# A cross-attention and MX-FFN kernel: a first pass over all batches, gate arithmetic once on 128 partitions, weight scaling on VectorE

## What is computed

```python
ig = (x @ Wi + bi); fg = (x @ Wf + bf)          # x = concat(q, k, v), per head
log_f_cum = cumsum(log_sigmoid(fg))
log_D = tril(log_f_cum[s] - log_f_cum[t]) + ig[t]
D = exp(log_D - max(log_D))
C = (q @ k.T / sqrt(dh)) * D
h = (C / (max(|C.sum(-1)|, exp(-max(log_D))) + EPS)) @ v
x = x + layernorm_per_head(h) * ln_scale
```

## Time and profile before

| | us |
|---|---|
| median of 3 runs (624.54 to 626.63) | 626.4 |
| the profiled execution, own time | 627.32 |
| its span, first to last instruction | 625.5 |
| start, to the first CT product | 38.5 |
| batch steps, to the end of the last CT product | 367.5 |
| from there to the first transpose of the FFN | 27.7 |
| FFN from there | 191.8 |

### The profile page before, as it was taken

How to read it: one execution, slowest core, us unless ns; L and a number is a source line. 1 busy time by engine, 2 the same in 40 slices (tenths; PEclk the granted TensorE clock), 3 DMA queues, 4 the chain that set the end, 5 groups by cost and what they waited for, 6 DMA issues and landing times.

```text
span 625.5 us, 10355 instructions
## 1 busy us (share of the span) xinstructions
PE 500.4 (80%) x2944; PEld 324.3 (52%) x2992; DVE 516.3 (83%) x759; ACT 379.1 (61%) x739; POOL 381.2 (61%) x359
## 2 busy tenths in 40 slices
PE   1768689679789779867868768457999999999994
PEld 1356575566566557745646565343444444444441
DVE  1257899999999999999999999947788888888882
ACT  2487786787877867867867876632333443343342
POOL 5456677778668758848858758763334344444443
PEclk9977877787777875878866957757999999999999
DMA  5330313212302312302311301001011111111120
GB/s 129 136 102 1 102 35 103 101 35 103 101 34 101 101 34 101 101 34 94 103 38 47 121 1 34 18 1 50 1 44 58 34 51 49 34 59 41 34 67 34
DMA packets 25479, 38.48 MB, mean 62 GB/s; under 512 B 4848, under 2 KB 8944, under 8 KB 25456
## 3 DMA queue, kind: packets, MB, share of 16 engines
q1 hardware_dynamic: 25456, 38.21, 18.8%
HBM read 29.82 MB, written 8.39 MB: 61 GB/s over the span
## 4 chain that ended last, share of the span: by engine, by line
PE 40%; DVE 33%; issue 13%; ACT 8%; POOL 4%; DVEq 1%; DMA 1%; POOLq 0%; ACTq 0%; SPq 0%
PE psA L1335 7%; PE psA L1344 7%; PE psC L1362 5%; PE psA L1171 4%; PE psA L1145 4%; DVE wam L887 3%; PE psC L1204 3%; PE psC L1113 3%; DVE CT L959 3%; DVE f L935 3%; DVE wn L915 2%; POOL wn L598 2%; PE psB L1354 2%; ACT Dt L694 2%; PE psC L1195 2%
## 5 line engine op out<-in xcount | busy, mean ns | idle before, releaser
L598 POOL TENSOR_TENSOR wn<-wq,ps 128x1024 bf16<-128x1024 bf16 x32 | 61.1, 1911 | 109.7 <-DVE wq L1088 109.7
L1171 PE MATMUL psA<-vp,CT 128*128 128x33 f32 x512 | 83.5, 321 | 24.3 <-DVE CT L959 24.1
L1171 PEld LDWEIGHTS psA<-vp,CT 128*128 128x128 f32 x512 | 80.6, 243 | 29.6 <-issue 15.5
L1145 PE MATMUL psA<-qbd,kT 128*128 128x512 f32 x128 | 71.6, 711 | 0.4 <-issue 0.4
L694 ACT ACTIVATE Dt<-psB,gT 128x128 f32<-128x128 f32 x256 | 70.9, 376 | 0.2
L494 POOL TENSOR_TENSOR wq<-wn,ws 128x1024 bf16<-128x1024 bf16 x24 | 45.9, 1911 | 38.4 <-DVE wn L916 38.4
L844 ACT ACTIVATE wy<-psB 128x1024 bf16<-128x1024 bf16 x32 | 32.7, 1023 | 59.1 <-PE psB L1354 58.5
L501 POOL TENSOR_TENSOR wy<-wm,wy 128x1024 f32<-128x1024 f32 x24 | 63.2, 2632 | 0.9 <-ACT wm L676 0.9
L1335 PE MATMUL psA<-WgT,xqT 128*128 128x512 bf16 x241 | 61.6, 395 | 2.3 <-ACT WdT L687 1.5
L1362 PE MATMUL psC<-WdT,wy 128*128 128x512 bf16 x248 | 60.1, 379 | 2.9 <-ACT wy L844 2.4
L1344 PE MATMUL psA<-WuT,xqT 128*128 128x512 bf16 x255 | 62.0, 386 | 0.2 <-issue 0.2
(11 more groups left out here) (130 smaller groups left out, 1103.3 us busy)
## 6 DMA issues: line engine op xcount, KB each, us to landing
xt<-in_x_dram SPq DMA_DIRECT2D x8, 512.0 KB, 4.8
ct<-in_ctx_dram SPq DMA_DIRECT2D x8, 512.0 KB, 3.4
wraw<-in_L_ffn_w_gate_dram SPq DMA_DIRECT2D x8, 512.0 KB, 4.1
wraw<-in_L_ffn_w_up_dram SPq DMA_DIRECT2D x8, 512.0 KB, 4.8
wraw<-in_L_ffn_w_down_dram SPq DMA_DIRECT2D x8, 512.0 KB, 3.8
xr<-in_x_dram SPq DMA_DIRECT2D x16, 256.0 KB, 2.7
x_scratch<-x SPq DMA_DIRECT2D x16, 256.0 KB, 2.1
wm<-x_scratch SPq DMA_DIRECT2D x16, 256.0 KB, 2.7
```

The source lines that it names most:

```text
L598: nc.gpsimd.tensor_tensor(blocks(pd[h][:, :]), blocks(pc[h][:, :]), spread(ps4[h][:, :], PB), ALU.mult).then_inc(pq_ready.sem, 1)
L1145: nc.tensor.matmul(psA[:, i4, :], kT[p][:, i4, c * P:(c + 1) * P], qbd[:, i4, :, :].rearrange("p j t -> p (j t)"), start=True, stop=True). ...
L1171: last = nc.tensor.matmul(psA[:, i4, j * VW:(j + 1) * VW], CT[n % 2][:, j * P:(j + 1) * P], vp[p][:, c, HPC * i4 + j, :], start=True, stop ...
```

## The change

Shapes, inputs and the FFN loop are the same. What changes is the attention stage:

- A first pass over all batches (`pre_step`) loads, normalises and transposes x and ctx, makes the gate products, and quantises one down-weight unit per batch. The transposed q and k of all batches stay in SBUF (qTa, kTa). x and ctx have two buffers each.
- `gates` now has tokens as output partitions: 16 products per batch with 32 columns (both gates of 16 heads). After the last batch the gates of all batches and heads are transposed once to 128 partitions (8 batches x 16 heads) x 256, and log-sigmoid, scans, split and exponentials run once on those. The split rows go through a DRAM scratch (gs_dram, 393 KB) and come back per batch as factors movt and statt in eight small transfers (`load_decay`); the carry factor goes through g5_dram (four transfers a batch, `load_carry`).
- A second pass (`step`) makes the eight score tiles. `qk` takes 16 products of 32 rows and 128 columns per chunk in place of the four block-diagonal ones, so qbd goes; the exponent of D comes from two products, including the part that was ScalarE's bias, so `exps` is one activation of 128x512. `inter` adds the state's part in PSUM with a scaled q (`carry_q`, on GpSimd), in place of `combine`. Head variance, norm, residual, statistics and rounding work on both chunks at once (128x1024). The reciprocal root of the head variance is one pow on GpSimd (128x32) in place of logarithm, exponential and a correction.
- Weight units: scaling and scaling back move to VectorE, the addition too (as part of two `scalar_tensor_tensor` of the rounding), the clamp is absorbed, and the rounding constant is one activation. GpSimd has no weight work left. Eight units are in the first pass, two in the gate stage, two per batch after that (gate and up).
- FFN buffers are parts of qTa and kTa.

The core of the diff, in the order GpSimd, ScalarE, VectorE, TensorE:

```diff
+        qTa = sb("qTa", [P, B, HC, S])
+        kTa = sb("kTa", [P, B, HC, S])
...
+            def carry_q(b):
+                gp.wait_ge(g5b_ld, 16 * HPC * b + 16 * HPC)
+                gp.wait_ge(inter_done.sem, inter_done.at(b, 0))
+                settle(gp)
+                nc.gpsimd.tensor_tensor(qs[:, :, :], qTa[:, b, :, P:S], g5b[:, :, :], ALU.mult).then_inc(qs_ready.sem, 1)
...
+            def head_rsqrt(b):
+                gp.wait_ge(hv_ready.sem, hv_ready.at(b, 1))
+                nc.gpsimd.tensor_tensor(sm[:, 4, :, :].rearrange("p c h -> p (c h)"),
+                                        sm[:, 3, :, :].rearrange("p c h -> p (c h)"), mhalf[:, :],
+                                        ALU.pow).then_inc(hr_ready.sem, 1)
...
+            def step(b, p, n, first, last):
+                if not first:
+                    head_rsqrt(b - 1)
+                    residual(b - 1)
+                    x1_rsqrt(b - 1)
+                if not last:
                     weigh(b + 1, 1 - p)
+                    carry_q(b + 1)
+                if not first:
+                    back_x(b - 1)
...
+            def round_const(w, p):
+                act.wait_ge(pow_ready.sem, pow_ready.unit(w))
+                nc.scalar.activation(wm[p][:, :], wm[p][:, :], ACT.Identity, scale=W_SLOPE,
+                                     bias=wbase[:, 0:1]).then_inc(m_ready.sem, 1)
...
+            def pre_step(b, p, n, first, last):
+                copy_T(b, 0)
+                copy_T(b, 1)
+                if not last:
+                    x_norm(b + 1, 1 - p)
+                round_const(b, p)
+                if not first:
+                    evac_down(b - 1, b - 1)
...
+            def step(b, p, n, first, last):
+                if not first:
+                    square(b - 1)
+                exps(b, 0)
+                exps(b, 1)
+                if not last:
                     copy_v(b + 1, 1 - p, 0)
...
+                exps(b, 2)
+                exps(b, 3)
+                evac_gate_up(2 * b + B + 1, 1, b)
+                if not last:
+                    round_const(2 * b + B + 2, 0)
+                exps(b, 4)
+                copy_h(b, 0)
+                if not first:
+                    x1_norm(b - 1)
+                exps(b, 5)
+                if not last:
...
                     copy_v(b + 1, 1 - p, 1)
+                exps(b, 6)
+                if not last:
+                    evac_gate_up(2 * b + B + 2, 0, b + 1)
+                exps(b, 7)
+                if not last:
                     copy_state(b + 1)
...
+                    round_const(2 * b + B + 3, 1)
+                copy_h(b, 1)
+                if not first:
+                    evac_xq(b - 1)
...
+            def w_front(w, p, n):
+                ve.wait_ge(w_ld[p], 16 * n + 16)
+                ch.link(reduce_blocks(blocks(wraw[p][:, :]), wam[p][:, :]))
+                ch.link(power(wam[p][:, :], ws4[p][:, :]))
+                ch.link(inverse(ws4[p][:, :], winv[p][:, :], INV_W))
+                nc.vector.tensor_tensor(blocks(wy[p][:, :]), blocks(wraw[p][:, :]), spread(winv[p][:, :], UB),
+                                        ALU.mult).then_inc(y_ready.sem, 1)
+
+            def w_pow(w, p):
+                ve.wait_ge(y_ready.sem, y_ready.unit(w))
+                nc.vector.tensor_scalar(wm[p][:, :].bitcast(I32), wy[p][:, :].bitcast(I32), EXPO, None,
+                                        ALU.bitwise_and).then_inc(pow_ready.sem, 1)
+
+            def w_round(w, p):
+                ve.wait_ge(m_ready.sem, m_ready.unit(w))
+                ch.link(nc.vector.scalar_tensor_tensor(out=wy[p][:, :], in0=wy[p][:, :], scalar=W_LOW, in1=wm[p][:, :],
+                                                       op0=ALU.max, op1=ALU.add))
+                ve.wait_ge(wT_mm.sem, wT_mm.unit_before(w, 2))
+                nc.vector.scalar_tensor_tensor(out=wq[p][:, :], in0=wy[p][:, :], scalar=W_HIGH, in1=wm[p][:, :],
+                                               op0=ALU.min, op1=ALU.subtract).then_inc(wn_ready.sem, 1)
+
+            def w_back(w, p):
+                ve.wait_ge(wn_ready.sem, wn_ready.unit(w))
+                nc.vector.tensor_tensor(blocks(wq[p][:, :]), blocks(wq[p][:, :]), spread(ws4[p][:, :], UB),
+                                        ALU.mult).then_inc(wq_ready.sem, 1)
...
+            def pre_step(b, p, n, first, last):
+                w_front(b, p, n)
+                if not first:
+                    w_round(b - 1, 1 - p)
+                if not last:
+                    x_stats(b + 1, *after(p, n))
+                if not first:
+                    w_back(b - 1, 1 - p)
+                w_pow(b, p)
...
+            def step(b, p, n, first, last):
+                if not last:
+                    w_front(2 * b + B + 2, 0, b + B // 2 + 1)
+                if not first:
+                    head_var(b - 1)
                 c_mult(b, 0)
                 c_mult(b, 1)
+                w_round(2 * b + B + 1, 1)
                 c_mult(b, 2)
+                if not first:
+                    head_norm(b - 1)
+                w_back(2 * b + B + 1, 1)
                 c_mult(b, 3)
+                if not last:
+                    w_pow(2 * b + B + 2, 0)
+                if not first:
+                    x1_stats(b - 1)
                 c_mult(b, 4)
+                if not last:
+                    w_front(2 * b + B + 3, 1, b + B // 2 + 1)
                 c_mult(b, 5)
+                if not last:
+                    w_round(2 * b + B + 2, 0)
+                if not first:
+                    x1_round(b - 1)
                 c_mult(b, 6)
+                if not last:
+                    w_back(2 * b + B + 2, 0)
                 c_mult(b, 7)
+                if not last:
+                    w_pow(2 * b + B + 3, 1)
...
+            def gates(b):
+                pe.wait_ge(tr_ev.sem, tr_ev.at(b, 2))
+                settle(pe)
+                for c in range(NCH):
+                    for k in range(2 * HC):
+                        src = (qTa if k < HC else kTa)[:, b, k % HC, c * P:(c + 1) * P]
+                        last = nc.tensor.matmul(gate_out[:, b, c, :], src, wgt[:, k, :], start=False,
+                                                stop=k == 2 * HC - 1, skip_group_check=True)
+                return last
...
+            def qk(b, c):
+                pe.wait_ge(h_ev.sem, h_ev.at(b, c))
+                settle(pe)
+                for i4 in range(HC):
+                    for j in range(HPC):
+                        r = slice(DH * j, DH * (j + 1))
+                        last = nc.tensor.matmul(psA[:, j, i4 * P:(i4 + 1) * P], kTa[r, b, i4, c * P:(c + 1) * P],
+                                                qTa[r, b, i4, c * P:(c + 1) * P], start=True, stop=True)
+                        if i4 == HC - 1:
+                            last.then_inc(qk_done.sem, 1)
...
+            def step(b, p, n, first, last):
+                qk(b, 0)
                 heads(b, p, 0)
+                decay(b, p, 2)
+                if not last:
+                    centre(b + 1, 0)
                 heads(b, p, 1)
+                decay(b, p, 3)
                 heads(b, p, 2)
+                decay(b, p, 4)
+                if not first:
+                    pe.wait_ge(xqT_ev.sem, xqT_ev.at(b - 1, 0))
+                w_transpose(2 * b + B + 1, 1, rows_order)
                 heads(b, p, 3)
+                decay(b, p, 5)
+                qk(b, 1)
+                if not last:
+                    centre(b + 1, 1)
                 heads(b, p, 4)
+                decay(b, p, 6)
                 heads(b, p, 5)
+                decay(b, p, 7)
+                if not last:
+                    w_transpose(2 * b + B + 2, 0, rows_order)
+                    state(b + 1)
                 heads(b, p, 6)
                 heads(b, p, 7)
+                inter(b)
+                if not first:
+                    pe.wait_ge(wT_ev.sem, wT_ev.unit(2 * b + B + (1 if last else 2)))
+                    x_transpose(b - 1)
+                if not last:
+                    decay(b + 1, 1 - p, 0)
+                    decay(b + 1, 1 - p, 1)
```

More of the change, by code:

```diff
@@ L1332, in gate @@
+            decay(0, 0, 0)
+            pe.wait_ge(gT_ev, 1)
+            decay(0, 0, 1)
+            for b in range(B):
+                step(b, b % 2, b // 2, b == 0, b == B - 1)
+            def gate(t, b, q, h):
                 pe.wait_ge(silu_done.sem, silu_done.at(t, h))
```

1464 lines of the change are left out of this document (651 added, 813 removed).

## The result

The changed kernel takes 681.2 us (median of 4, 677.0 to 682.4), the kernel before 626.2 beside it: ratio 1.087, 95% interval 1.082 to 1.092. The profiled execution took 681.3 us with a span of 679.5. Some executions of a kernel fell in a slower state, and every median and ratio is of the others. The forecast was 645 (595 to 675): slower was right, the size was not. Of 55 us, 19 were foreseen.

What follows compares the result with a forecast made beforehand. VectorE was taken to bound the old steps, TensorE the FFN loop. First CT product 115, step 0 to 139, six steps to 398, last to 432, tail to 452, FFN to 644; plus 1.8, less 0.9: 645 us (595 to 675).

Steps and rivals of the forecast that it cites:

- step 0: First second-pass step: 24 us, from CT 0 to CT 7 without head norm, statistics, rounding or an earlier batch's boundary.
- the walk: Steady second-pass step followed through the engines' lists from the end of CT product 7, 0.1 us per handover: CT 7 at 42.6.
- Rival A: Second pass: the batch boundary does not stall, a step falls to 35 us; total 590 us, chance 0.33.
- the half-clock term: Steady second-pass step: 0.9 us added to 42.6 for TensorE partly at half clock, giving 43.5 us.
- three pieces of 0.8: Steady step: heads cost 0.8 us more each at half clock (1.86 for 1.03), reaching the chain three times.
- The tail: From the last CT product to the first FFN transpose: 20 us, against 27.7 before.
- power 1: After the last CT product: the head variance's power on GpSimd counted as 1 us.
- The paragraph on the rule and the row: GpSimd's 128x32 pow: 5.2 us at 0.15 a column; a skill rule says it blocks VectorE, a profile row says not.
- Rival B: Second pass: the pow takes 5.2 us and holds the port, CT 2 2.6 later seven times; 663 us, chance 0.10.
- the row L941: Earlier profile: a VectorE scan reading SBUF twice took its usual 0.68 us inside a GpSimd pow, so a pow blocks nobody.
- Rival C: Second pass: qk's 32-row products run one after another, 8.3 us at half clock; step 49, total 681 us, chance 0.06.
- Rival D: First pass: TensorE at half clock bounds it, 12.0 us a batch, 16 us more; total 664 us, chance 0.05.

Runs made afterwards that it cites:

- The run with 28 fillers: Changed kernel plus 28 unread 128x512 bf16 products per step on TensorE, 20 ahead of the gate weights' transpose, 8 ahead of x_transpose: 677.4 us.
- The single edits: Each alone on the changed kernel: back_x ahead of carry_q, 672.3 us; power replaced by multiplication, 674.0; exps 7 ahead of gate weights' eviction, 677.1; ln_scale on VectorE, 683.7.

## Why the prediction was off

| step of the prediction | forecast | measured |
|---|---|---|
| first CT product ends | 115 | 118.0 |
| step 0 | 24 | 28.3 |
| the next six steps | 259 | 273.1 |
| last step | 34 | 36.6 |
| last CT product to the first FFN transpose | 20 | 29.0 |
| FFN | 192 | 194.5 |

**The mechanism held.** The first pass costs its whole length and the steps can't give it back, since their boundary stalls. VectorE's idle stretches are where the walk had them, and its busy share, 66%, is the forecast's 65%; there luck helped, since both sides of it were low, 30.6 us of 46.2 where 27.5 of 43.5 had been counted. Rival A, "the batch boundary does not stall", fell. With another order and less on GpSimd a step takes 36.3 us, near A's 35, so what A lacked was lists that fit the work, though that kernel's work is no longer quite the one that A counted. The first CT product was 3 us late, as much as it moves between executions.

**The step that failed is the half-clock term**, "42.6 + 0.9". The forecast took TensorE's clock from 0.73 and 0.62 in the earlier trace rows; it was 0.53 in the second pass, so nearly every product ran at the lower of the two levels. The forecast's three pieces of 0.8 come to 2.4 there, not 0.9, and they are not all of it. Held against the walk, from the end of CT 7 at 281.18: CT 1 ended at 14.1 (12.9), CT 2 at 20.5 (17.6), CT 4 at 30.9 (27.6), CT 7 at 46.3 (42.6). Of the 3.7 us, 2.9 are there at CT 2. Up to CT 0 TensorE does heads 7 and inter (1.93, where 1.0 was taken), which ends at 3.8 instead of 2.3. From CT 0 to CT 2 the walk had 5.3 us and the trace 7.0, and TensorE does heads 0, a decay pair, the centring one behind the other, at a clock of 0.50:

```profile
294.86 1.89 PE L1227 MATMUL psA<-vp,CT 128*128 128x33 f32 x8 [1.51 <-DVE CT L981]
296.56 0.61 PE L1216 MATMUL psB<-mask,identb 128*128 128x512 bf16 x1
297.11 0.60 PE L1218 MATMUL psB<-movt,statt 32*128 32x512 bf16 x1
297.64 2.08 PE L1184 MATMUL psC<-cen,kTa 128*128 128x128 f32 x8
```

The run with 28 fillers tests it: there the same heads of the same step took 1.05, CT 2 waited 2.0 to 2.1 us in three steps where it had waited 2.5 to 3.2, and at a clock of 0.66 the period was 1.7 us shorter. What the step would take at the full level, no run showed. In step 0, 4.3 us over its forecast, TensorE works without a gap from 118.11 to 131.85, at 0.50, and CT 4 waits 6.97 us; that all of the 4.3 is the clock's was not tested.

**In GpSimd's part** the ln_scale product took 3.26 us and not the 2.35 taken from L501, and w_pow beside it 2.24 (that kind of slowing stands in the earlier trace rows). It cost little: with ln_scale moved away CT 4 came no earlier. Others of VectorE's work grew too: it was busy 30.6 us of a step where 27.5 had been counted.

**The tail** was mis-sized by 9 us, half of it in one place: "power 1". The paragraph on the rule and the row had 5.2 for the same power, and it was hidden only in the steps; at the end it stood bare:

```profile
471.48 1.23 DVE L1002 TENSOR_TENSOR early<-hf,sm 128x1024 f32<-128x1024 f32 x1 [5.54 <-POOL sm L579]
```

Without the power that wait was 0.36, and a step was no shorter. L1083, beside GpSimd's residual, took 3.12 instead of 1.23 (another 1.9), and inter, copy and square 7.9 instead of 6, with heads 6 and 7 (3.62) and inter (1.93) ahead at half clock.

**Rival B fell**: the power took 5.43 us eight times, as 0.15 a column had said, and held nothing: both roundings ran inside the power of 340.34 to 345.77 at their usual length.

```profile
340.34 5.43 POOL L579 TENSOR_TENSOR sm<-sm,mhalf 128x32 f32<-128x32 f32 x1 [5.59 <-DVE sm L997]
```

```profile
341.56 1.22 DVE L905 SCALAR_TENSOR_TENSOR wy<-wy,wm 128x1024 f32<-128x1024 f32 x1
342.90 1.23 DVE L908 SCALAR_TENSOR_TENSOR wq<-wy,wm 128x1024 bf16<-128x1024 f32 x1
```

So for this pair the row L941 was right. The rule of the Trainium skill ("SBUF — State Buffer", "SBUF: two separate sides"), by which such a pair excludes each other for the whole instruction, did not hold here: L905 reads two SBUF tiles and took 1.22. **Rival C fell**: 16 products of 32 rows took 2.09 us at half clock, a quarter of 8.3. Its number, 681, came true for another reason. **Rival D fell**: a batch of the first pass took 9.6 us (one L905 at 54.31, the next at 63.96), against 9.3 forecast and D's 12.0. Two sums there were slips: 16 us more than 645 are 661 and not 664, and four times 1.86 are 7.4 and not 7.2 for the gate products.

**The single edits** taught less than expected. Each took away a wait that was there, and the period moved between 1.3 us less and 0.7 more. Where one wait went another grew: without ln_scale on GpSimd the one at CT 4 went from 0.78 to 2.79. This fits two chains of nearly the same length, TensorE's list at half clock on one side, square, power, residual and rounding on the other, but no run measured the length of either alone.

## What to carry to other kernels

Work that is woven into the gaps of a loop can cost little. Here, put in a pass of its own, it cost its full length, and the loop gave that back only when its lists had a new order for the work that was left and GpSimd had less to do. When each single edit moves a wait to another place, change the order and the relief together before judging either. Count every long instruction twice, once in the loop where it is covered and once at the end where it is bare.

## What the runs showed of the hardware

- 24 scalings of 128x1024 f32, moved from GpSimd to VectorE (1.25 us each), cost 29.9 us of VectorE's time and freed 42.2; the kernel's time did not fall.
- What slowed a neighbour was the operation and not that GpSimd was busy: beside a two-input product or sum on GpSimd, the VectorE passes read above took 2.24 to 3.27 us instead of 0.68 to 1.23; beside the power, 1.22 and 1.23.
- The granted clock was 0.53 over the second pass, where TensorE was busy 74%, and 0.62 in the last stretch before the FFN in the earlier trace rows, busy 62%. With fillers it was 0.59 at 86% and 0.66 at 87%. So the clock of one stretch could not be read off the busy share of another, as the forecast did. Why it was 0.53, no run showed.
